# Four graph passes: TensorE's signals moved from matmuls to drains and its sequencer

## The reference

```python
def _hypergraph_conv(x, hei, W, b, ...):      # 106,250 edges (src, he), sorted by he
    xw = x @ W.T
    edge_feat = b_inv[:, None] * segment_sum(xw[src], he)
    out = d_inv[:, None] * segment_sum(edge_feat[he], src)
    return out + b
```

## Time and profile before

| | |
|---|---|
| time, median of 3 runs | 6879.01 us (6859.34 to 6892.88) |
| span of the profiled execution | 6729.2 us |
| profiled execution's own time | not given beside its span; the median is 149.8 us above the span |
| PE busy, share of the span | 4418.9 us, 66% |
| POOL busy | 3355.7 us, 50% |
| DVE busy | 2669.2 us, 40% |
| ACT busy | 1559.4 us, 23% |
| mean granted PE clock | 0.812 |
| the four passes | some 60 to 4004 us of the span |

### The profile page before, as it was taken

How to read it: one execution, slowest core, us unless ns; L and a number is a source line. 1 busy time by engine, 2 the same in 40 slices (tenths; PEclk the granted TensorE clock), 3 DMA queues, 4 the chain that set the end, 5 groups by cost and what they waited for, 6 DMA issues and landing times. The chain is left out here.

```text
span 6729.2 us, 72351 instructions
## 1 busy us (share of the span) xinstructions
PE 4418.9 (66%) x20150; PEld 3518.5 (52%) x20150; DVE 2669.2 (40%) x6797; ACT 1559.4 (23%) x3386; POOL 3355.7 (50%) x3423
## 2 busy tenths in 40 slices
PE   3611139766778867876766659998546666666399
PEld 2410027554666646665555549996424444444287
DVE  7610026322222221112444342225566666666544
ACT  1100025212232222322222224333300000001233
POOL 5677730555455555655544421112466666662555
PEclk8755569878888888987888879998767777777599
DMA  7800024435444445555555550710554444444255
GB/s 265 255 18 11 11 62 120 123 107 167 128 134 131 133 148 158 162 149 167 166 166 161 154 159 0 201 38 4 147 139 117 119 118 121 118 120 118 100 88 88
DMA packets 523908, 822.38 MB, mean 122 GB/s; under 512 B 92040, under 2 KB 428367, under 8 KB 520055
## 3 DMA queue, kind: packets, MB, share of 16 engines
q0 software_dynamic: 158784, 367.62, 21.0%
q1 hardware_dynamic: 269235, 331.42, 16.5%
q10 hardware_dynamic: 95588, 120.03, 5.5%
HBM read 658.73 MB, written 198.82 MB: 127 GB/s over the span
## 5 line engine op out<-in xcount | busy, mean ns | idle before, releaser
L1072 PE MATMUL s_part<-both_halves,s_ring 128*128 128x512 f32 x4704 | 1330.9, 441 | 934.8 <-issue 467.3
L519 POOL DMA_INDIRECT acc<-table,ids x1296 | 1265.4, 976 | 1050.5 <-PE s_part L1043 634.7
L1072 PEld LDWEIGHTS s_part<-both_halves,s_ring 128*128 128x128 f32 x4704 | 984.3, 214 | 1217.9 <-issue 559.7
L1953 POOL DMA_INDIRECT at_rows<-h_t,ids x832 | 807.8, 971 | 470.4 <-issue 249.1
L1056 PE MATMUL s_part<-acc 128*128 128x257 f32 x3456 | 907.8, 411 | 148.5 <-DMA acc<-table,ids 59.0
L1056 PEld LDWEIGHTS s_part<-acc 128*128 128x128 f32 x3456 | 707.7, 210 | 278.2 <-DMA acc<-table,ids 64.8
L621 ACT ACTIVATE s_ring<-acc 128x896 fp32r<-128x896 bf16 x672 | 612.1, 945 | 886.3 <-remote 329.6
L519 POOL DMA_INDIRECT acc<-xn_d,ids x432 | 431.6, 999 | 495.3 <-PE s_part L1043 338.6
L2358 PE MATMUL at_part<-at_rows,at_onehot 128*128 128x264 f32 x1664 | 604.6, 493 | 4.1 <-DVE at_onehot L2175 4.1
L725 DVE TENSOR_TENSOR acc<-acc 128x256 f32<-128x256 f32 x96 | 40.9, 426 | 1376.9 <-ACT acc L662 1376.3
L528 POOL DMA_INDIRECT counted<-acc,s_place x416 | 427.2, 1027 | 132.0 <-issue 128.6
(11 more groups left out here) (418 smaller groups left out, 6172.7 us busy)
## 6 DMA issues: line engine op xcount, KB each, us to landing
acc<-counted SPq DMA_DIRECT2D x672, 224.0 KB
xs_d<-blank SPq DMA_DIRECT2D x38, 1032.0 KB
counted<-in_x ACTq DMA_DIRECT2D x24, 1568.0 KB
table<-acc ACTq DMA_DIRECT2D x214, 128.0 KB
acc<-table,ids POOLq DMA_INDIRECT x1299
both_halves<-table SPq DMA_DIRECT2D x21, 896.0 KB, 11.9
ex_x<-xs_d SPq DMA_DIRECT2D x60, 258.0 KB
at_rows<-h_t,ids POOLq DMA_INDIRECT x832
```

The lines of the kernel that those rows point to most:

```text
L519: pool.indirect_dma_start(rows[:, j % R, k, 0:D], None, table[0:NP_, :], bass.IndirectOffsetOnAxis(cst["ids"][:, t:t + 1], 0)).then_inc(ro ...
L1072: ins = pe.matmul(part[i % 4][:], chunk(n)[:, b * P:(b + 1) * P].bitcast(F32R), both[:, c * BG + b].bitcast(F32R), start=(c == 0 and b == ...
L1953: pool.indirect_dma_start(rows[:, t % AHEAD, :], None, table, bass.IndirectOffsetOnAxis(cst["ids"][:, t:t + 1], 0)).then_inc(rows_in[t % A ...
```

## The change

In the four passes no matmul increments a semaphore any more. PE issues a `drain` (an instruction of its sequencer that ends when the engine is idle), which carries one increment; the other increments are `sem_inc` instructions of the sequencer behind it. There is one drain at the end of each chunk, with `a_used`, and one at the end of each group, with `group_done`, now behind the opening of the next group where that is opened there. `freed`, `made`, `column_out` and `turned` follow the group's drain, or the drain of chunk 3 of a D. Three items at the end of a pass have a drain each.

```diff
@@ turn, column_of, make @@
-                    ins = pe.transpose(psT[b][:, h * P:(h + 1) * P], frm[:, h * P:(h + 1) * P], cst["ident"][:])
-                ins.then_inc(turned, 1)
+                    pe.transpose(psT[b][:, h * P:(h + 1) * P], frm[:, h * P:(h + 1) * P], cst["ident"][:])
-                pe.matmul(psY[:, D:D + 1], total_sum, cst["ones"][:, 0:1], start=True, stop=True).then_inc(column_out, 1)
+                pe.matmul(psY[:, D:D + 1], total_sum, cst["ones"][:, 0:1], start=True, stop=True)
-                    ins = pe.matmul(psY[:, 0:D], turned_x[k % 2][:, h, :], w[:, h, :], start=(h == 0), stop=(h == 1))
-                ins.then_inc(made, 1)
+                    pe.matmul(psY[:, 0:D], turned_x[k % 2][:, h, :], w[:, h, :], start=(h == 0), stop=(h == 1))
+            def made_and_turned(i, narrow=True):
+                if makes and i >= 3:
+                    pe.sem_inc(made, 1)
+                    if with_column(i - 3) and narrow:
+                        pe.sem_inc(column_out, 1)
+                if turns and LAG <= i < NI + LAG:
+                    pe.sem_inc(turned, 1)
@@ groups_of_tiles @@
-                    ins.then_inc(freed, 1)
                 open_sum(0, at_g[0])
+                pe.drain().then_inc(freed, 1)
...
                         if k and i - at_g[k - 1] > 3:
                             open_sum(k, i)
+                            pe.drain().then_inc(freed, 1)
...
-                        ins.then_inc(group_done, 1)
-                        if k + 1 < GS and at_g[k + 1] - i <= 3:
+                        opens = k + 1 < GS and at_g[k + 1] - i <= 3
+                        if opens:
                             open_sum(k + 1, at_g[k + 1])
+                        pe.drain().then_inc(group_done, 1)
+                        if opens:
+                            pe.sem_inc(freed, 1)
+                        made_and_turned(i)
...
-                            ins.then_inc(a_used, 1)
+                            pe.drain().then_inc(a_used, 1)
+                            if c == NG // 2:
+                                made_and_turned(i)
                 for i in range(NI, NI + 3):
                     make_and_turn(i)
+                    pe.drain()
+                    made_and_turned(i)
```

More of the change, by code:

```diff
@@ L1042, in open_sum @@
                     frm = rows[:, (j - 1) % R, JT - 1]
-                    ins = pe.matmul(part[i % 4][:, 0:D + 1], sel[:, j % OG, :], frm[:, 0:D + 1], start=True, stop=False)
-                    ins.then_inc(freed, 1)
+                    pe.matmul(part[i % 4][:, 0:D + 1], sel[:, j % OG, :], frm[:, 0:D + 1], start=True, stop=False)
                 open_sum(0, at_g[0])
+                pe.drain().then_inc(freed, 1)
                 for i in range(NI):
@@ L1055, in groups_of_tiles @@
                                 make_and_turn(i)
-                            ins = pe.matmul(part[i % 4][:, 0:D + 1], onehot[:, k % OG, t, :], rows[:, k % R, t, 0:D + 1],
-                                            start=False, stop=(t == JT - 1))
-                        ins.then_inc(group_done, 1)
-                        if k + 1 < GS and at_g[k + 1] - i <= 3:
+                            pe.matmul(part[i % 4][:, 0:D + 1], onehot[:, k % OG, t, :], rows[:, k % R, t, 0:D + 1],
+                                      start=False, stop=(t == JT - 1))
+                        opens = k + 1 < GS and at_g[k + 1] - i <= 3
+                        if opens:
                             open_sum(k + 1, at_g[k + 1])
+                        pe.drain().then_inc(group_done, 1)
+                        if opens:
+                            pe.sem_inc(freed, 1)
+                        made_and_turned(i)
                     else:
@@ L1071, in groups_of_tiles @@
                             for b in range(BG):
-                                ins = pe.matmul(part[i % 4][:], chunk(n)[:, b * P:(b + 1) * P].bitcast(F32R),
-                                                both[:, c * BG + b].bitcast(F32R), start=(c == 0 and b == 0),
-                                                stop=(c == NG - 1 and b == BG - 1))
-                            ins.then_inc(a_used, 1)
+                                pe.matmul(part[i % 4][:], chunk(n)[:, b * P:(b + 1) * P].bitcast(F32R),
+                                          both[:, c * BG + b].bitcast(F32R), start=(c == 0 and b == 0),
+                                          stop=(c == NG - 1 and b == BG - 1))
+                            pe.drain().then_inc(a_used, 1)
+                            if c == NG // 2:
+                                made_and_turned(i)
                 for i in range(NI, NI + 3):
                     make_and_turn(i)
+                    pe.drain()
+                    made_and_turned(i)
             def tiles_alone():
@@ L1116, in tiles_alone @@
                                 make_and_turn(i, False)
+                                pe.drain()
+                                made_and_turned(i, False)
                             if n % NG < NG - 1:
```

## The result

The changed kernel takes 7425.9 us (7422.7 to 7432.3, 4 runs), the kernel before beside it 6885.9 (6859.3 to 6897.5, 4 runs): a ratio of 1.079, with a 95% interval of 1.0766 to 1.0814, or 540 us more. The forecast was 7105, in a range up to 7300: the sign was right, the size was not.

A forecast was written before the change was run, and what follows sets the result against it. A loop of TensorE, ACT and POOL, TensorE with most work, was taken as the bound. Drains 236 + 85 us and sequencer increments 32 make 353, times 0.64 is 226, added to the 6879.0 median: 7105 us, range 6750 to 7300.

The forecast's parts named there:

- What bounds the passes: Four passes: a loop of TensorE, ACT and POOL, TensorE with most work; its increments seem to arrive late.
- The increments removed, 0 us: Taking 1518 increments off matmuls in the passes gains 0 us; the skill's rule would give 40 us less.
- The price of a drain, 0.44 us: Each exposed drain behind a chunk or group costs TensorE 0.44 us, between 0.34 and 0.54: 236 and 85 us.
- How much reaches the end, 0.64: Of 353 us added on TensorE in the passes, its busy share of 64% reaches the end: 226 us.
- The worst case of the prediction: Upper bound for the passes: 0.54 us a drain, all passed on, and ACT late: 394 + 32 + 48 = 474 us.
- What it moves, 0 to 48 us: `turned` and `made` come half an item later: 0, at most 48 us over 96 D items; `group_done`, `freed` 0.
- the sequencer's increments: 625 increments between drain and next matmul in the passes, 0.051 us each, not hidden: 32 us.
- the cured case: Rival: prompt signals to ACT and POOL remove three quarters of TensorE's idle time in passes 2 to 4: 6709 us, chance 0.25.
- drains last microseconds with no matmul under way: Sign in the later profile that the forecast is wrong: the delay would sit in the completion; no size given.
- Hidden: Rival: POOL and chunk landings set the passes, or cure and price cancel; no change, 6880 us, chance 0.13.
- The clock falls: Rival: holes between chunks lower the granted clock in the passes by a tenth more: 7300 us, chance 0.07.
- Signs in the trace: 905 drains, count matmuls 0.25 to 0.27 us, longer POOL waits, passes 2 to 4 50 to 100 us longer, later stages unchanged.

The follow-up runs named there:

- the deeper ring: Kernel before with 4 buffers of widened chunks in place of 3 and 6 landing buffers in place of 7: 6748.7 us, ratio 0.9847.
- its run of the last row: The changed kernel run again unaltered, beside the kernel before at 6732.8 us: 7308.3 us, ratio 1.0856.

## Why the prediction was right or wrong

**What bounds the passes: right.** A loop of TensorE and ACT, and late increments in it. That the lateness of the earlier trace rows costs time, and is not only in the records, is supported by two things: the kernel before with one gather takes 1058 us less for the same matmuls (POOL's work went too), and the deeper ring gains 106 us with all gathers and 21 without most. It shows in TensorE's signals and not in ScalarE's: from the end of ScalarE's copy of a sum to VectorE's next start on it (L734, L725) the median is 0.11 us in the kernel before and 0.10 us with one gather.

**The increments removed, 0 us: not contradicted.** No run removed increments alone. By the rule of the Trainium skill (TensorE: Matmul & The Clock Gate, "The cost: per-tile semaphore tail") taking them off would have saved an estimated 40 us. With nearly the same drains, the kernel that keeps all increments on matmuls has a ratio of 1.0621 and the one without them 1.079, so no run shows such a gain.

**The price of a drain, 0.44 us: right where it was read, a little high.** With one gather a group it is 0.41 us with the increments behind it, 0.39 in passes 2 to 4. Between two chunks with nothing between them it can be read by itself: in these traces a chunk starts 1.96 us after the one before it with drains and 1.60 us without (medians), 0.36 us more. Seven matmuls take 1.87 us between drains, as counted, and the next chunk starts 0.08 us behind their modelled end, in place of 0.15. Ahead of an item's turned and made parts it is more, 0.34 us:

```profile
1099.56 1.87 PE L1083 MATMUL s_part<-both_halves,s_ring 128*128 128x512 f32 x7
...
1101.77 0.35 PE L1010 MATMUL s_psY<-ones,acc 128*128 128x1 f32 x2 [0.34 <-issue]
```

**The step that failed first: that the price of a drain holds in the stretches with gathers.** Even with no drain hidden the forecast's own price makes 905 x 0.44 + 32 = 430 us, 110 less than the 540 measured. The change costs 370 us with one gather a group and 170 more with all. The drain was costed from the rows of other stages, where it ends 0.05 us behind the last matmul. In the passes 236 of 906 end microseconds late. The prediction had the mechanism in one clause, as an argument against a rival ("or in the completion itself, and then the drain waits for it too and TensorE stops, where today it runs on"), gave it no price and no chance. From the earlier trace rows, with one stop of 3.73 us behind five chunks, an estimate would have been 905 / 5 x 3.73 = 675 us of late ends; it was 1437. Of these far less, some 170 us if no drain was hidden, came on top of what the kernel before took. That late ends are what adds the 170 us was not tested apart from all else that the gathers change (the granted clock of passes 2 to 4 is 0.80 to 0.83 with them and 0.97 without most). Why it is so little I put down to the fact, not tested by itself, that the kernel before waited for the same completions through ACT and in "issue" (466.6 and 467.3 us). Pass 1 fits that: with one gather a group its late ends beside the scatters come to 319 us, and the changed kernel's pass 1 is only 96 us longer than that of the kernel before, for 227 drains.

**How much reaches the end, 0.64: wrong too, by as much as these runs show.** It was made from TensorE's busy share, as if its idle time were cover. Without most of the gathers 370 us reached the end, where 905 x 0.36 + 32 = 358 us would be the whole price. That is no test where TensorE is busy 94% of the time, but in pass 1 it is busy 53% there (719.75 of 1367 us), and the drains still cost 96 / 227 = 0.42 us each. So 314 us are missing (540 - 226): if nothing was hidden with all gathers either, 144 of them belong to this step and 170 to the one above; if a part was hidden, the one above has more. The worst case of the prediction, 474 us, ends at 7353; the range was cut at 7300, and even that case is below 540.

**What it moves, 0 to 48 us: at its bound.** Alone it costs 0.63%, 43 us. Drains alone and moved signals alone make 428 + 43 = 471 of 540 us; for the sequencer's increments 32 us were forecast and never measured, and how the other 69 us are split is open. **Slips in the sums:** 432 gathers at 0.98 and 0.30 us are 553 us, not some 540; and the 265 us of the cured case are not the price with every drain exposed, which is 666 x 0.44 = 293 us and the increments. Neither changes the forecast.

**Rivals.** *Cured* fell: the delay sits in the completion, as the test "drains last microseconds with no matmul under way" says, as far as modelled ends go. *Hidden* fell. *The clock falls*: it did, in passes 2 to 4 from 0.87, 0.88 and 0.82 to 0.83, 0.82 and 0.80, but it is a small part. TensorE's busy time grew by 227 us over the passes; between the two kernels with one gather it grew by 2461 - 2254 = 208 us (sums over their four passes) at nearly the same clock (0.94 to 0.97 in passes 2 to 4), so the matmuls that start anew behind each drain can account for nearly all of it. **Signs in the trace**: the 905 drains are there, as forecast; count matmuls take 0.267 us where they run undisturbed, but 1499.6 / 4704 = 0.32 us over all, above the 0.25 to 0.27 of the forecast; POOL's waits for `freed` grew from 634.7 to 1179.4 us, as forecast in kind; the passes grew by 120 to 210 us, trace to trace, against 40 to 100; the stages behind grew by 32 us, trace to trace, with TensorE's busy time the same to 3 us.

## What to carry to other kernels

Price a drain, or any step at which an engine must be idle, in the stretch where it will stand and not where one is found: here it cost 0.4 us beside quiet neighbours, and with all gathers one in four ended late, by 6 us on average, and the whole change cost 170 us more. Do not discount such a step by the busy share of its engine: in a pass with TensorE 53% busy the whole price reached the end. If increments already arrive late in a trace, an instruction that waits for completion turns a late signal into a stopped engine; more buffers between the engines helped with the first (1.5% here) and did nothing for the second. Here the increment was better left on the matmul.

## What had not been expected of the hardware

- While GpSimd issues indirect gathers (1728 in the passes, 0.98 us each), TensorE's completions are late by microseconds again and again: 236 of 906 drains, 1437 us in all, the longest drain 61 us; with one gather a group 24 drains and 370 us, most of it beside GpSimd's 416 scatters. A quarter of the columns (1457 us late) and an eighth of the rows (1544 us) leave it, and so does an eighth of the chunk loads (1454 us). The largest late ends come back at the same drains: the 36th and the 43rd of pass 1 end 41.0 and 41.8 us late in the changed kernel, 41.4 and 42.0 in its run of the last row, 41.6 and 41.0 with one gather a group.
- The lateness is not in proportion to the number of gathers: 370, 526 and 1437 us with one, four and eight tiles gathered a group. Why a gather instruction holds TensorE's completions up, and why short gathers cost more time than full ones, stays open. The fetching of the program is not it, as far as the trace shows: a packet of instructions lands within only 24 of 235 late ends. Every run has its span and granted clock on record, so none tells whether the delay is there when nothing is recorded.
- The kernel before took 6715 to 6888 us from one row of runs to another, each within 0.8%, while the changed one took 7308 and 7426 in two of them. Each row of experiments ran on another chip; whether the chip makes the difference was not tried.
